# Four groups of instructions moved in a hand-ordered two-block model

## The reference

```python
x = L0_attn_x                                   # (8, 512, 256)
xn = _layernorm(x)
s = retention(xn, ln_w, ln_b, Wq, Wk, Wv, Wg, g_norm_w, Wo)       # 4 heads, chunks of 64
g = _silu(windowed_ffn(xn, wqkv, ..., wo, w1, b1, w2, b2))        # 2 layers, see below
x = x + s * g
xn = _layernorm(x)
s = latent_attention(xn, W_DQ, W_UQ, W_QR, W_DKV, W_UK, W_UV, W_KR, W_O)   # 16 heads, causal
g = _silu(mixture(xn, gate_w, w1, w2))                            # top 2 of 8 experts
x = x + s * g

def _layer(x, ...):                             # one of the 2 layers of windowed_ffn
    q, k, v = split(shift_token(x) @ wqkv)      # 8 heads of 64
    q, k = rotary(l2norm(q) * qs, l2norm(k) * ksc)
    x = x + local_attention(q, k, v) @ wo       # softmax over this and the previous 128 keys
    h = layernorm(shift_token(x)) * lg + lb
    a, g = split(h @ w1 + b1)
    return x + (a * gelu(g)) @ w2 + b2

def latent_attention(x, ...):
    c_q, c_kv = x @ W_DQ, x @ W_DKV
    Q = concat(c_q @ W_UQ, rope(c_q @ W_QR)); K = concat(c_kv @ W_UK, rope(x @ W_KR))
    scores = where(causal, clip(Q @ K.T, -80, 80), -inf)
    return softmax(scores / sqrt(24)) @ (c_kv @ W_UV) @ W_O
```

## Time and profile before

| | us |
|---|---|
| median of 3 runs | 2995.11 |
| the 3 runs | 2986.7, 2997.85, 2995.11 |
| the profiled execution | 2986.93 |
| its span, first to last instruction | 2984.8 |

### The profile page before, as it was taken

The page is one execution under the profiler, slowest core; times in us unless marked ns, Lnnn a source line. Parts: engine busy times, 40 slices in busy tenths (PEclk is TensorE's granted clock), DMA queues, the critical chain, the costliest instruction groups (busy, mean ns, idle before and its releaser), DMA issues.

```text
span 2984.8 us, 41964 instructions
## 1 busy us (share of the span) xinstructions
PE 2747.3 (92%) x15582; PEld 1858.1 (62%) x15582; DVE 1538.1 (52%) x3722; ACT 1229.7 (41%) x2281; POOL 1058.8 (35%) x734
## 2 busy tenths in 40 slices
PE   6999999999999999899999899999988899999992
PEld 4575656656575656556565555555554488888992
DVE  6555556565555547576666667575754521000003
ACT  4444444535344444444444545454533242222221
POOL 5424243342424244252534435353622221111113
PEclk8999999999999999999999999999998799999996
DMA  3000000000001011001010101010000367989986
GB/s 137 11 23 18 25 28 26 15 25 15 25 24 47 26 57 50 15 4 50 4 50 4 50 4 50 4 43 12 29 33 29 142 255 280 346 336 346 334 328 206
DMA packets 85907, 261.83 MB, mean 88 GB/s; under 512 B 10668, under 2 KB 49916, under 8 KB 67020
## 3 DMA queue, kind: packets, MB, share of 16 engines
q1 hardware_dynamic: 79228, 241.38, 22.3%
q0 software_dynamic: 6480, 17.77, 1.6%
HBM read 210.81 MB, written 44.11 MB: 85 GB/s over the span
## 4 chain that ended last, share of the span: by engine, by line
PE 77%; DVE 9%; DMA 5%; ACT 3%; issue 2%; POOL 2%; SPq 1%; POOLq 0%; DVEq 0%; ACTq 0%
PE s_pD L708 20%; PE s_pA L708 19%; PE s_pD L1160 8%; PE s_pA L1145 7%; PE s_pD L862 4%; PE s_pD L780 3%; PE s_pA L758 3%; PE s_pA L767 3%; DMA s_w_w<-rows_s 2%; PE s_pA L747 2%; PE s_pA L872 2%; DVE s_pairs L1736 2%; DMA s_z<-s_cur 1%; PE s_pA L719 1%; DVE s_qk L1640 1%
## 5 line engine op out<-in xcount | busy, mean ns | idle before, releaser
L1471 POOL TENSOR_TENSOR s_qk<-s_qk,s_rrec 128x1024 f32<-128x1024 f32 (+1 forms) x128 | 220.9, 1726 | 602.5 <-DVE s_rrec L1646 602.4
L708 PE MATMUL s_pA<-s_w_wqkv,s_curT 128*128 128x512 f32 x768 | 353.8, 601 | 5.6 <-ACT s_curT L1190 3.7
L708 PEld LDWEIGHTS s_pA<-s_w_wqkv,s_curT 128*128 128x128 f32 x768 | 142.2, 191 | 176.3 <-issue 162.8
L1214 ACT ACTIVATE s_qk<-s_qk,s_mx 128x256 f32<-128x256 f32 (+1 forms) x512 | 239.8, 471 | 27.7 <-DVE s_mx L1640 27.0
L1736 DVE TENSOR_SCALAR s_pairs<-s_pD 128x1024 f32<-128x1024 f32 (+1 forms) x192 | 194.3, 1039 | 108.5 <-PE s_pD L862 107.5
L2088 DVE COPY s_w_wo<-s_pD 128x256 f32<-128x256 f32 x71 | 30.0, 423 | 409.4 <-PE s_pD L1131 409.4
L1561 POOL DMA_INDIRECT acc_s<-s_w_w,s_sq x71 | 68.4, 963 | 468.5 <-ACT s_w_w L1413 461.1
L1465 POOL TENSOR_TENSOR s_rinv<-s_ssq,s_half 128x16 f32<-128x16 f32 x64 | 220.5, 3445 | 0.0
L862 PE MATMUL s_pD<-s_mixer 32*128 32x512 f32 (+3 forms) x1024 | 186.2, 477 | 32.9 <-DVE s_pairs L1736 20.4
L1430 POOL TENSOR_TENSOR s_rs<-s_ve,s_half 128x4 f32<-128x4 f32 x40 | 43.3, 1083 | 441.5 <-DVE s_ve L1602 441.5
L1284 ACT ACTIVATE s_pairs<-s_pairs 128x2560 f32<-128x2560 f32 x64 | 149.6, 2338 | 94.9 <-DVE s_pairs L1736 94.9
(11 more groups left out here) (269 smaller groups left out, 5775.9 us busy)
## 6 DMA issues: line engine op xcount, KB each, us to landing
s_qkT<-in_m_w SPq DMA_DIRECT2D x48, 1024.0 KB, 5.2
s_v_tm<-in_m_w SPq DMA_DIRECT2D x24, 1024.0 KB
s_rot<-in_m_w SPq DMA_DIRECT2D x24, 1024.0 KB, 5.6
s_w_wqkv<-in_m_w SPq DMA_DIRECT2D x23, 1024.0 KB
s_qk<-in_m_w SPq DMA_DIRECT2D x23, 1024.0 KB, 5.3
s_w_w<-rows_s SPq DMA_DIRECT2D x71, 129.0 KB
s_cur<-in_x SPq DMA_DIRECT2D x8, 512.0 KB, 3.5
xn_s<-s_cur SPq DMA_DIRECT2D x8, 512.0 KB, 2.6
```

The source lines that it names most:

```text
L708: last = nc.tensor.matmul(out, lhs(c), rhs(c), start=(c == 0), stop=(c == n - 1))
L1214: last = nc.scalar.activation(pi, pi, ACT.Exp, scale=-1.0, bias=mx[:, u, i:i + 1], accum_out=rsum[:, u, i:i + 1])
L1471: nc.gpsimd.tensor_tensor(pi, pi, rrec[:, u, :].unsqueeze(2).broadcast_to((P, 4, 256 - lo)), ALU.mult).then_inc(p_rdy, 1)
```

## The change

No instruction is added or removed, and none changes its shape. Four groups move.

1. Retention stages 0 to 5: `input_stats(k + 2)` and POOL's root for it move from step 8 to step 10, directly ahead of `input_apply(k + 2)`.
2. Retention stages 0 to 7: half 1 of the down projection, and DVE's residual for it, move from step 1 to step 2; on PE it then stands behind the turning of step 0. `PT_even`, into which ACT copies that turning, is also one of the tiles the down projection reads, so ACT's copy now waits until half 1 has been multiplied.
3. Latent stages 8 to 14: on DVE `gated_sum(b, 1)` goes ahead of the reciprocal of step 3, with its statistics (now `tokens_stats`) behind that reciprocal and ahead of `local_out`; `tokens_shift` goes ahead of the reciprocal of step 4. PE's x1T transposes and ACT's `tokens_in` go ahead of the turning and its copy in step 5. In steps 6 and 8 `keys_queries` goes ahead of the turning and values on PE, ahead of the values in ring D, and ahead of `local_out` on DVE.
4. Latent stages 9 to 14: on ACT `latent_exp(b - 1, 6)` moves from behind the v copy of product 2 to behind that of product 3.

```diff
@@ ring_a_jobs
+            if s.lat and u == 5:
+                j += [("x1T", b, 0), ("x1T", b, 1)]
             if s.ahead and 2 <= u < 2 * NT + 2:
                 j += [("PT", k + 1, u - 2)]
...
@@ ring_d_jobs
+            if s.lat and not s.last and u in (6, 8):
+                j += head(b, u // 2 - 2)
             if s.ahead and u >= 3:
                 j += [("O", k + 1, u - 3)]
...
-            if (s.ret or s.last) and u == 1:
+            if s.last and u == 1:
                 j += [("w2", k, 0), ("w2", k, 1)]
-            if s.lat and not s.last and u in (1, 2):
+            if s.here and not s.last and u in (1, 2):
                 j += [("w2", k, u - 1)]
@@ PE
-                    if s.ahead and 2 <= u < 2 * NT + 2:
-                        local_transposes(k + 1, u - 2)
+                    if s.lat and not s.last and u in (6, 8):
+                        keys_queries(b, u // 2 - 2)
                     if s.lat and u == 5:
                         for i in range(2):
                             pe.wait_ge(norm_x, NT * b + 2 * i + 2)
                             pair_transposes("x1T", b, i, lambda t, c: xn[:, t, c * P:(c + 1) * P])
+                    if s.ahead and 2 <= u < 2 * NT + 2:
+                        local_transposes(k + 1, u - 2)
...
                         down_projection(k, 0)
-                        if s.ret or s.last:
+                        if s.last:
                             down_projection(k, 1)
-                    if s.lat and not s.last and u == 2:
+                    if s.here and not s.last and u == 2:
                         down_projection(k, 1)
@@ ACT
                 ps = takeA("PT", b, w)
+                if w == 0 and 1 <= b <= B:
+                    act.wait_ge(mmD, DJ["w2", b - 1, 1] + 1)
...
-                    if s.behind and t < (2 if s.last else 3):
+                    if s.behind and t < 2:
                         latent_exp(b - 1, 4 + t)
+                    if s.behind and t == 3 and not s.last:
+                        latent_exp(b - 1, 6)
...
+                    if s.lat and u == 5:
+                        tokens_in(b, 0)
+                        tokens_in(b, 1)
                     if s.ahead and 2 <= u < 2 * NT + 2:
                         local_turned(k + 1, u - 2)
@@ POOL
-                    if s.ret and k + 2 < B and u == 8:
+                    if s.ret and k + 2 < B and u == 10:
                         reciprocal_roots(var_1, rstd_1, k + 2)
@@ DVE
                         local_max(k + 1, u)
+                    if s.lat and not s.last and u == 3:
+                        gated_sum(b, 1)
+                    if s.lat and not s.last and u == 4:
+                        tokens_shift(b)
                     if s.ahead and 1 <= u < 2 * NT + 1:
                         local_reciprocal(k + 1, u - 1)
+                    if s.lat and not s.last and u == 3:
+                        tokens_stats(b, 1)
+                        ln_variances(var_x)
...
+                    if s.lat and not s.last and u in (6, 8):
+                        keys_queries(b, u // 2 - 2)
                     if s.ahead and u >= 3:
                         local_out(k + 1, u - 3)
-                    if s.ret and u == 1:
-                        ffn_out(k, 0)
-                        ffn_out(k, 1)
+                    if s.ret and u in (1, 2):
+                        ffn_out(k, u - 1)
...
-                    if s.ret and k + 2 < B and u == 8:
-                        input_stats(k + 2)
                     if s.ret and u == 10:
                         ret_out(k, 0)
                     if s.ret and k + 2 < B and u == 10:
+                        input_stats(k + 2)
                         input_apply(k + 2)
```

More of the change, by code:

```diff
@@ L146, in ring_a_jobs @@
                 j += [("roT", k, u // 2 - 3)]
-            if s.lat and u == 5:
-                j += [("x1T", b, 0), ("x1T", b, 1)]
             if s.lat and u == 5:
@@ L220, in ring_d_jobs @@
                 j += [("rank", b)]
-            if s.lat and u in (6, 8):
+            if s.last and u in (6, 8):
                 j += head(b, u // 2 - 2)
@@ L1355, in _ @@
                         tokens_norm(b)
-                    if s.lat and u == 5:
-                        tokens_in(b, 0)
-                        tokens_in(b, 1)
                     if s.ahead and u < 2 * NT:
@@ L1698, in gated_sum, with tokens_stats @@
                 dve.wait_ge(x1_rdy, 2 * b + i + 1)
+            def tokens_stats(b, i):
                 for t in range(2 * i, 2 * i + 2):
@@ L2027, in _ @@
                         gated_sum(b, 0)
+                        tokens_stats(b, 0)
                     if s.lat and u == (1 if s.last else 2):
                         ffn_out(k, 1)
-                    if s.lat and u == (2 if s.last else 3):
+                    if s.last and u == 2:
                         gated_sum(b, 1)
+                        tokens_stats(b, 1)
                         ln_variances(var_x)
@@ L2036, in _ @@
                         latent_out(b - 1, u - 3)
-                    if s.lat and not s.last and u == 4:
-                        tokens_shift(b)
                     if s.last and u == 5:
```

## The result

The changed kernel takes 2946.0 us in the median of 4 runs (2945.0 to 2950.0), the kernel before 2990.9 (4 runs, 2979.9 to 2997.9). The ratio of the two is 0.9856, with a 95% interval of 0.9821 to 0.9890: 43 us (33 to 54) less. The forecast was 2943, in the range 2918 to 2973. The time was right, but partly by luck: of the terms of the sum part 4 had the wrong sign, the keys and the clock gave more than was forecast, and the two errors cancelled.

The account below looks back on a forecast made before the run. PE was taken to set the pace, so only its waits and low clock could be won: 9.0 + 2.4 + 26 + 4.2 + 4.8 + 2 = 48 us off 2991.7 gave 2943 us, range 2918 to 2973.

Parts of the forecast that it names:

- part 4: Stages 9 to 14: moving the exponential removes PE's 1.6 us zT wait; 0.8 a stage reaches the end, 4.8 us.
- the keys: Latent stages: PE's 0.9 us wait at the latent scores goes, 0.6 kept, seven times, 4.2 us.
- the clock: Latent stages: fewer and shorter PE waits leave fewer half-clock stretches; 2 us off in all, ends 0 and 24.
- part 1: Retention stages 0 to 5: PE's 1.5 us wait at a value product goes, six times, 9.0 us.
- part 2: Retention stages: waits of 1.1 and 0.5 merge into about 1.3; 0.34 won seven times, 2.4 us.
- part 3: Latent stages, gated sum, shift and x1T: PE's waits fall from 6.1 to 2.4 us, seven times, 26 us.
- the rival of late statistics: Retention stages' end: the apply comes 1.2 us late, so part 1 gives 2 instead of 9; 2950 us, chance 0.10.
- the cluster: PE's waits from step 3 to the latent projections of a latent stage, 6.1 us together, forecast to fall to 2.4.
- rival 3: Latent stages: the half-clock stretches go with the idle, another 22 us off; 2921 us, chance 0.12.
- Rival 1: Latent stages: the cluster gives 15 instead of 26 us, part 4 nothing, POOL being the bound; 2960 us, chance 0.24.
- rival 4: Slower: merged wait in retention stages or new turning wait in latent ones lets the clock fall; 3010 us, chance 0.04.

Follow-up runs that it names:

- e1: The changed kernel with part 4 undone (ACT's exponential of pair 6 behind the v copy of product 2 again); ratio to the kernel before 0.9814.
- e2: The kernel before with part 4 alone (ACT's exponential of pair 6 moved); ratio to the kernel before 1.0071.
- e9: The kernel before with gated sum, shift and x1T of part 3 moved, without the keys and queries; ratio to the kernel before 0.9890.
- e4: The changed kernel with POOL's mask of pair 6 behind product 3's head norms, not ahead of product 2's rotary sum; ratio to the kernel before 0.9805.
- e3: The changed kernel with POOL's mask of pair 6 behind product 2's head norms, not ahead of its rotary sum; ratio to the kernel before 0.9801.
- e6: The kernel before with part 2 alone (half 1 of the down projection behind the turning); ratio to the kernel before 0.9992.
- e12: The kernel before, with no edit, profiled once more; one run each, 2991.5 us beside 2987.2.
- e7: The kernel before with only the gated sum of part 3 moved ahead of the reciprocal of step 3, its statistics split off; ratio to the kernel before 0.9973.

## Why the prediction was right, and where it was not

By timed ratios, in us of 2990: a part alone against before, except part 4, which is after against e1. Each has an uncertainty of 4 to 12, so part 4's 13 is just clear of nothing by this pair; e2 against before gives 21 (15 to 27).

| step | forecast | measured, timed | rest alone, stages named |
|---|---|---|---|
| part 1 | -9.0 | -9 | -9.6 (0 to 5) |
| part 2 | -2.4 | -2 | -2.8 (0 to 6) |
| part 3, sum, shift, x1T | -26 | -33 | -17.4 (9 to 14) |
| part 3, keys | -4.2 | -17 | -6.7 (9 to 14) |
| part 4 | -4.8 | +13 (e2: +21) | +9.4 (9 to 14) |
| clock | -2 | in the rows above | |
| all | -48 | -43 | |

- **Part 1 and the rival of late statistics.** Right in size and mechanism. The slack was 0.36 us; the bound of the apply at 355.5 was too careful.
- **Part 2.** Right by the trace: the one merged wait, at 1.4, was forecast at 1.3. The timed runs alone can't show so small a gain.
- **Part 3.** The waits left in the cluster came out as worked out (2.3 against 2.4), the product at 0.69, the new wait for POOL in place. 3.7 a stage was forecast, 2.9 of rest came in e9. The term was too large because its 6.1 was read in one stage (k = 11); the mean of stages 9 to 14 was 5.2, and 5.2 - 2.3 is the 2.9. Its timed 33 us are above the 26 by half clock, as far as its one trace shows (17.2 against 30.3). The keys' estimate of 0.6 a stage was too low: 1.1 arrived, since there was a second wait of 0.32 that the earlier trace rows don't list, and the bank I held against it cost nothing that the sum shows.
- **Part 4 is the step that failed.** The prediction saw that POOL's mask slips with the exponential and priced that at 0.6 against the 1.6 won. The slip itself was nearly right (0.8 at the mask, 0.9 at the sum behind it). But the prediction counted the slip against the first turning, some 45 us later, and not against the rotary sum that stands right behind the mask in POOL's queue. Nor did it see that DVE's rotary products would come 1.7 earlier with the removed wait. The two met: 3.44 us instead of 1.28, and 2.9 to 3.5 of waiting at the gate in place of the 1.6. Its ceiling of 1.05, for the first turning, was not the one met first either: with POOL's order mended (e4) 1.2 of the 1.6 comes back at the gate. I had weighed just this clash of POOL and DVE for line 1693 (2.29 beside 0.69), by the Trainium skill's sentence on the port that the two share ("GPSIMD Engine Reference", Specifications), and did not ask which other pair of two-input instructions the change would bring together. e1 and e2 show the loss with and without the other parts, e3 and e4 that it comes by POOL's order.
- **The clock's term was too small.** 2 us were forecast. The half clock of stages 9 to 14 went from 30.3 to 25.3 in after, which is inside the 23 to 31 of the unchanged stages and shows no gain by itself, and to 17.1, 16.5 and 14.1 in e1, e3 and e4, below that range. For e1 the 13 us lie midway between the forecast and rival 3 (24 in all). A part of the difference between after and e1 can be placed: in each of the stages 9 to 14 of after one half-clock stretch starts from 0.4 us before to 0.9 us behind the end of the wait at the gate. The small idles named in the Trainium skill ("TensorE: Matmul & The Clock Gate", A second HAM failure mode) fit the direction: PE waits 63 us in stages 9 to 14 of before and 42 in e1, with 30.3 and 17.1 of half clock; but e6 has 63 us of waits there too and only 22.9, so 7 us of half clock come and go without a change.
- **Rival 1** forecast 2960 by a smaller gain of the cluster and nothing for part 4; the cluster's 2.9 a stage lies between its 2.1 and the forecast's 3.7, and part 4 was worse than nothing. That the time is far from 2960 is owed to the keys and the half clock. The slower side (rival 4) did not come: retention stages 1 to 5 stayed at 1.00 with a merged wait of 1.4. Stage 6 fell to 0.99 and was 0.9 us longer than before, but it was longer in e12, the unchanged kernel, too (135.5 against 134.0).

So the total was met by luck, because part 3 and the keys, with the half clock that went with them, gave some 20 us more than forecast, and part 4 took 18 more. The reference also mattered: against the profiled execution of before alone I would have said 2939.

## What to carry to other kernels

When an instruction is moved on one engine, follow what depends on it to the queues of the other engines, and look at what stands right behind the waiting one there: here a slip of 0.9 us on POOL, and DVE's coming 1.7 us earlier once the wait was gone, changed which instructions of the two run side by side, and that cost more than the wait removed. Price a removed wait at its mean over all stages, not at one stage's, less what is late next, and then check the neighbours of every moved start for such a pair. Compare versions stage by stage and separate half clock from the rest, since the profiles of one kernel differ by more than a small part of a change is worth.

## What was not expected of the hardware

- Two DVE products of 128x512 took 3.44 us beside a POOL sum of 128x1024 and 1.28 without it; one of them took up to 2842 ns against a middle of 684. POOL's sum was slowed less, from 2.35 to 2.85.
- Half clock cost an untouched stage (9) about 3.1 us in e12 and 6.8 in the first profile of before.
- With an untouched second part of the program, what follows stage 15's start took from 757.1 (e4) to 775.7 us (e7).
